# A two-layer decoder on one core: start-up loads reordered, first-batch rotary sums on VectorE, one projection step moved, and a new merge of the lanes

## Chip, cores and metric

One core of one Trainium2 chip. The metric is device time in microseconds (us) of one launch; the runs before are given as the median of 3. The engines are named as in the profile: PE is TensorE's matrix multiplication, PEld its weight load, DVE is VectorE, ACT is ScalarE, POOL is GpSimd, SP is SyncE; SPq and ACTq are the DMA issues of SP and ACT.

## What is computed

The input is 16 sequences (batches) of 256 tokens by 256 channels, float32, and a context of the same shape. Six residual blocks follow one another, each ended by a layer norm without weights:

```
x = LN(x + attention_16_heads_with_rotary(x))       # layer 0, attention 0
x = LN(x + mLSTM_like_mixer(q=x, k=ctx, v=ctx))     # gates, decay matrix, 8 heads
x = LN(x + bitlinear_ffn(x))                        # ternary weights, 8-bit activations
x = LN(x + attention_16_heads(x))                   # layer 1, attention 1
x = LN(x + cross_attention_16_heads(x, ctx, ctx))   # attention 2
x = LN(x + relu_ffn(x))
```

The rotary part turns each pair (x1, x2) of a head into (x1*cos - x2*sin, x1*sin + x2*cos). The ternary weights are made on the chip from float32 ones: each is divided by the mean of its absolute values, rounded, and clipped to -1, 0, 1.

## The kernel before

**Lanes.** The 16 sequences are spread over 4 lanes (L0 to L3), four batches to a lane, one after the other. Each lane has its own buffers; a fifth lane, SETUP, holds the start-up work that all share. One sequence is a fixed list of steps, written in `lane_steps()`: `ctx` and `xT` turn the context and the stream (PE transposes into PSUM, ACT copies out), `rope` projects queries and keys and multiplies them by cos and sin on DVE, `qk` splits them into two half-precision parts, `stack` reads them back stacked from DRAM, `max` makes the scores and DVE takes their row maxima (line 1170), `negmax` turns the maxima, `exp` makes the scores again and ACT exponentiates (line 999), `pv` multiplies by the values, `heads` turns the result, DVE normalizes it (lines 1181 and 1183), `oT` turns it back, `proj` projects it, and `norm` ends the block. A name is written here with its attention and its unit: `max 0.3 L2` is the fourth unit of attention 0 in lane 2.

**Order.** Every engine runs one list, a merge of the lanes' lists. The merges are written out by hand of a planner as strings of digits (`TURNS`, one digit a step, the lane that is next) and the PSUM bank of every PE result stands in `PLACES`. `engine_program()` reads them. Each engine waits on semaphores and takes its own steps strictly in order, so a step that isn't ready holds all that stand behind it, on SP too, which issues nearly all DMAs. `nth()` gives the count of a semaphore at which a step of a lane is done.

**Start.** SP issues the constants, then stream and context of the lanes by turns with the first weights between them, then waits for the context of lane 2 (`sp.wait_ge(c_loaded[2], 16)`), then issues the raw weights of the ternary layer (3 MB), the bias rows, and three weights of layer 1. ACT issues, before any of its steps, four DMAs that preset a slot of `heads_dram` (lines 940 to 942), and starts its steps only behind them. DVE sums the raw weights (`sums`, line 1123), makes the scales (`scales`, lines 1126 to 1131), the ternary values (`ternary`, lines 1137 to 1141) and the masks. SP's steps `weights 0` to `weights 4` load the other weights; each of 0 to 3 first waits for both stacks of the lane of its number, and they have 6, 8, 9 and 14 DMAs.

**First batch, order before.** Decoded from `TURNS`, with the steps of batch 0:

- SP behind the first loads: qk 0.0 L0, stack 0.0 L0, qk 0.1 L0, qk 0.0 L2, stack 0.1 L0, stack 0.0 L2, qk 0.0 L1, qk 0.1 L2, stack 0.0 L1, qk 0.1 L1, qk 0.0 L3, stack 0.1 L2, stack 0.1 L1, weights 0, weights 1, weights 2, stack 0.0 L3, qk 0.1 L3, negmax L0, stack 0.1 L3, negmax L2, negmax L1, weights 3, negmax L3, weights 4.
- PE: ctx L0, xT L0, v L0, ctx L3, xT L3, ctx L1, xT L1, rope 0 L0, rope 1 L0, ctx L2, xT L2, ... rope 0 L3, sums, rope 1 L3 ...
- DVE: rope 0 L0, rope 1 L0, sums, rope 0 L2, rope 0 L1, rope 1 L2, qk 0 L0, qk 1 L0, rope 1 L1, rope 0 L3, rope 1 L3, scales, qk 0 L2, ternary 2, qk 0 L1, qk 1 L1, qk 1 L2, max 0 L0 ... max 7 L3 (with the two qk of L3 between), ternary 0, ternary 1, masks, heads L0.

**Rotary sums.** DVE writes the products (line 1145, 128x512 each, two for each unit of 128 tokens). POOL adds them crosswise, in two instructions of 128x256 a unit (line 1340), into `R`, a view of the key buffer; 8 units in the first batch of the four lanes, 32 in all. POOL also adds a bias row to the stream once a block (`xb`, line 1345).

**Second attention of layer 1.** `v 2` (the values of the cross attention, from the context) stands behind `proj 1`; on DVE it waits for the last `pv` of attention 1, whose values lie in the same buffer.

Of the kernel before, what the change touches and what calls it, by code (L numbers as in the profile page):

```python
# [12 lines left out]
ALU = mybir.AluOpType  # L13
# [44 lines left out]
def lane_steps():  # L58
# [6 lines left out]
    def attention(a):  # L65
# [17 lines left out]
        if a == 1:  # L83
            add("qk", 2, 1)
            add("stack", 2, 1)
        add("oT", a)
# [3 lines left out]
        if a == 1:  # L90
            add("v", 2)
# [51 lines left out]
def lane_program(lane):  # L143
# [7 lines left out]
    for at in range(-1, batches):  # L151
        for name, occ, unit, ahead in lane_steps():
            it = at + ahead
            if 0 <= it < batches and (at >= 0 or ahead):
                out.append((it, name, lane, occ, unit))
# [6 lines left out]
        "0003311002231122200134322110000300302201120222211112121331323033033000103020222002022032022033023303"  # L162
        "3320123033211301011320110313102123013203012223100323123121233302231302302330211313111200000110100311"
        "3330213223123020232233302301001001120010102313310020031130132100330220002302120302303323003231310333"
        "0213233221213022132312202100232021023100112011120113013213233101030131030132021003222121322032303332"
        "0201203231130101101103100023220010003112130222320121312313300323311301310003002323202332000122100100"
        "2002222030133302033120133011321012022122312103011023330213330130330023030031100113211011022122322322"
        "3111211023311021132112311021002301303230332212321322130120301011222111111032232333300300230103013031"
        "3212022022003033200002010330131103211223103012333100332112332132023330213223321303123212212122311322"
        "0120200202302102110131231121031132312330100310110010010201223212230303203203213331231011100210130200"  # L170
        "2130320030110212113022021312333123002110323002103100303320320023123222100100022000322201330102233033"
        "1113113022122021213320101302332013303133300030230011132010113110021222322232132321321112011120331103"
        "1233121203231010023203132131022031201211220111321210003102333132013130100330332022202210030233120030"
        "1210001123013021002130321302123132023330233133232312131310323221230230220200232001232012212200210103"
# [1223 lines left out]
```

## Time and profile before

| what | value |
|---|---|
| median of 3 runs | 1826.56 us (1825.21 to 1827.41) |
| the profiled execution's own time | 1808.41 us |
| its span | 1806.7 us |
| PE busy | 1552.5 us, 86% of the span |
| DVE busy | 1180.4 us, 65% |
| ACT busy | 967.1 us, 54% |
| POOL busy | 227.1 us, 13% |
| mean granted TensorE clock | 0.962 of full speed |

All durations below are those of the profiled execution, counted from the start of its span. An "[idle before <-releaser]" names how long an engine had nothing to run before the row and what ended that wait. The share of PE is high in the mean, but the first 110 us are unlike the rest.

### The profile page before, as it was taken

What the parts mean: (1) busy time and instruction counts of PE and PEld (TensorE: products, weight loads), DVE (VectorE), ACT (ScalarE), POOL (GpSimd) and SP (SyncE); (2) the same over time, 40 slices, a digit from 0 to 9 for tenths busy, and PEclk for the clock granted to TensorE, in tenths of its full rate; (3) what the DMA queues carried; (4) which work ended last, traced back from release to release, by engine and by line L of the source; (5) the groups of instructions that cost most, each with busy time, mean ns of one, the idle gap of its engine ahead of it and who ended that gap; (6) DMA issues with size and microseconds to landing.
All of it is one profiled execution on the core that took longest, in us unless ns stands there. A gap on an engine that the chain in (4) does not pass through costs nothing. (4 is left out here: it accounts for less than half of the span.)

```text
span 1806.7 us, 31811 instructions
## 1 busy us (share of the span) xinstructions
PE 1552.5 (86%) x12524; PEld 998.1 (55%) x12546; DVE 1180.4 (65%) x2087; ACT 967.1 (54%) x1717; POOL 227.1 (13%) x233
## 2 busy tenths in 40 slices
PE   6389788879998887889999897888999989698898
PEld 4146455546664554545676465545566546464467
DVE  4856897664465678676447678876355668886732
ACT  2077554655435755456534664645544566555562
POOL 5200110002111011000122011000012111100000
PEclk9579899999999989999999999999999999999999
DMA  6610023221221011422122001232123101123200
GB/s 216 185 60 1 1 88 97 83 68 42 67 75 48 1 42 42 123 63 74 59 65 74 28 7 46 80 95 83 33 71 96 58 2 42 41 82 104 63 1 24
DMA packets 115748, 114.36 MB, mean 63 GB/s; under 512 B 10515, under 2 KB 101395, under 8 KB 115603
## 3 DMA queue, kind: packets, MB, share of 16 engines
q1 hardware_dynamic: 115282, 111.28, 20.1%
q8 instruction: 103, 1.69, 0.4%
q10 hardware_dynamic: 320, 1.05, 0.3%
q14 instruction: 43, 0.34, 0.1%
HBM read 68.91 MB, written 42.99 MB: 62 GB/s over the span
## 5 line engine op out<-in xcount | busy, mean ns | idle before, releaser
L1170 DVE TENSOR_REDUCE nm<-psum 128x4 f16<-128x1024 f32 x384 | 458.3, 1224 | 125.0 <-PE psum L760 123.0
L999 ACT ACTIVATE PB<-psum 128x1024 f32<-128x1024 f32 x384 | 383.9, 1023 | 229.5 <-PE psum L797 120.3
L1345 POOL TENSOR_TENSOR XO<-XO,row_b 128x512 f32<-128x512 f32 x80 | 101.5, 1276 | 1176.9 <-ACT XT L970 1155.6
L797 PE MATMUL psum<-PB,V 128*32 128x256 f32 x3072 | 211.5, 395 | 10.4 <-ACT PB L999 7.3
L760 PE MATMUL psum<-QK 48*128 48x256 f16 x1536 | 148.6, 288 | 77.2 <-DMA QK<-heads_dram 23.6
L779 PE MATMUL psum<-QK 49*128 49x256 f16 x1536 | 147.0, 280 | 42.5 <-ACT PB L999 20.4
L760 PEld LDWEIGHTS psum<-QK 48*128 48x128 f16 x1536 | 55.2, 97 | 166.5 <-issue 70.7
L797 PEld LDWEIGHTS psum<-PB,V 128*32 128x32 f32 x3072 | 84.5, 111 | 87.7 <-issue 36.8
L779 PEld LDWEIGHTS psum<-QK 49*128 49x128 f16 x1536 | 52.6, 95 | 137.8 <-issue 53.3
L924 PE MATMUL psum<-XT,W 128*128 128x256 f32 x512 | 120.1, 384 | 0.0
L932 PE MATMUL psum<-W,PB 128*128 128x256 f32 x512 | 116.7, 383 | 0.0
L1003 ACT ACTIVATE U<-psum 128x512 f32<-128x512 f32 x128 | 76.0, 596 | 55.4 <-PE psum L797 35.4
L924 PEld LDWEIGHTS psum<-XT,W 128*128 128x128 f32 x512 | 94.6, 190 | 18.7 <-issue 6.3
L932 PEld LDWEIGHTS psum<-W,PB 128*128 128x128 f32 x512 | 95.6, 190 | 16.5 <-issue 4.2
L1111 DVE TENSOR_SCALAR XO<-Y,mv,rstd 128x256 f32<-128x256 f32 x192 | 73.4, 426 | 43.2 <-ACT rstd L954 43.2
L687 PE MATMUL psum<-W_o,XT 128*128 128x256 f32 x384 | 96.3, 394 | 3.1 <-ACT XT L1006 1.8
L1340 POOL TENSOR_TENSOR QK<-PB 128x256 f32<-128x256 f32 x64 | 74.9, 1198 | 150.1 <-DVE PB L1145 150.0
L1083 ACT ACTIVATE PB<-psum,col_b 128x256 f32<-128x256 f32 x128 | 53.5, 471 | 73.0 <-PE psum L924 72.7
L674 PE MATMUL psum<-cst,XO 128*128 128x128 f32 x512 | 82.7, 286 | 10.6 <-DVE XO L1111 5.5
L1229 DVE SCALAR_TENSOR_TENSOR PB<-psum,PB 128x768 f32<-128x768 f32 x64 | 60.7, 953 | 42.2 <-PE psum L864 41.7
L687 PEld LDWEIGHTS psum<-W_o,XT 128*128 128x128 f32 x384 | 70.2, 192 | 20.7 <-issue 7.4
L1189 DVE TENSOR_TENSOR Y<-psum,XO 128x512 f32<-128x512 f32 x48 | 33.1, 689 | 71.5 <-PE psum L687 44.2
(158 smaller groups left out, 2582.6 us busy)
## 6 DMA issues: line engine op xcount, KB each, us to landing
QK<-heads_dram SPq DMA_DIRECT2D x96, 512.0 KB, 3.6
heads_dram<-U SPq DMA_DIRECT2D x288, 128.0 KB, 2.0
XO<-in_x SPq DMA_DIRECT2D x16, 256.0 KB, 3.3
Y<-in_ctx SPq DMA_DIRECT2D x16, 256.0 KB, 3.4
out<-XO SPq DMA_DIRECT2D x16, 256.0 KB, 3.4
W<-in_w SPq DMA_DIRECT2D x2, 1024.0 KB, 7.6
QK<-GN SPq DMA_DIRECT2D x96, 4.0 KB
heads_dram<-QK ACTq DMA_DIRECT2D x4, 256.0 KB, 9.1
```

Of the source, the lines that this page charges most:

```text
L674: ins = pe.transpose(bank[:, k * TOK + t * P:k * TOK + t * P + P], src[:, t, k * P:(k + 1) * P], ident)
L687: ins = pe.matmul(bank[:, t * DIM:(t + 1) * DIM], xt(k)[:, t * P:(t + 1) * P], w[:, k], start=(k == 0), stop=(k == n - 1))
L760: ins = pe.matmul(b[:, e * 512 + t * TOK:e * 512 + (t + 1) * TOK], QS[L][r, unit, t * P:(t + 1) * P], KS[L][r, unit, :], start=True, stop= ...
L779: ins = pe.matmul(b[:, e * 512 + t * TOK:e * 512 + (t + 1) * TOK], KS[L][r, unit, t * P:(t + 1) * P], QS[L][r, unit, :], start=True, stop= ...
L797: ins = pe.matmul(b[SLOT * j:SLOT * j + SLOT, at:at + TOK], value(L, t, PAIRS * e + u, HEADS, HD, SLOT), src, start=(t == 0), stop=(t == T ...
L924: ins = pe.matmul(b[:, m * TOK:(m + 1) * TOK], W_1[:, k, c:c + P], XT_[L][:, k, :], start=(k == 0), stop=(k == KT - 1))
L932: ins = pe.matmul(b[:, 0:DIM], hid1(L, k)[:, unit * P:(unit + 1) * P], W_2[:, k], start=(k == 0), stop=(k == IT - 1))
L999: act.activation(PB[L][:, unit % PBUF, :], b[:, 0:1024], ACT.Exp, scale=HD ** -0.5)\
L1003: act.activation(flat2(U[L][:, unit - 1:unit + 1, :]), b[:, 0:512], ACT.Copy).then_inc(u_ready[L], 1)
L1170: dve.tensor_reduce(nm[L][:, :, :, unit].rearrange("p t e -> p e t"), b[:, 0:1024].rearrange("p (e t k) -> p e t k", e=2, t=TT), AX.X, ALU ...
L1340: pool.tensor_tensor(both[:, two], plain[:, two], crossed[:, 1 - two], ALU.add).then_inc(rot[L], 1)
L1345: pool.tensor_tensor(stream(L, it), stream(L, it), row_b[:, occ:occ + 1, :].to_broadcast([P, TT, DIM]), ALU.add).then_inc(xb_ready[L], 1)
```

## The change

It has these parts:

- `first()` loads all four streams ahead of all four contexts, waits for the stream of lane 3 in place of the context of lane 2, and waits for two memsets of POOL (`set_pool` at 2).
- The four presets of `heads_dram` are issued by SP there, ahead of the raw weights, and no longer by ACT.
- In what runs ahead of batch 0, the `ctx` steps stand at the end, behind the stacks; `nth()` counts accordingly.
- For batch 0, DVE makes the rotary sums itself, right behind the products of the unit, and POOL skips them. Later batches are as before.
- `v 2` stands ahead of `oT 1` and `proj 1`, behind `stack 2.1`.
- `TURNS` and `PLACES` are replaced by a new merge with as many steps on each engine (PE 1905, ACT 1377, DVE 1014, SP 294, POOL 192).

```diff
         if a == 1:
             add("qk", 2, 1)
             add("stack", 2, 1)
+            add("v", 2)
         add("oT", a)
         if a == 2:
             add("loadx", 0, 0, 1)
         add("proj", a)
-        if a == 1:
-            add("v", 2)
...
-        for name, occ, unit, ahead in lane_steps():
+        steps = lane_steps()
+        if at < 0:
+
+            steps.sort(key=lambda step: step[0] == "ctx")
+        for name, occ, unit, ahead in steps:
...
+    if it == 0 and what in ("ctx", "xT0"):
+        return 1 + (what == "ctx")
     return it * len(signals) + signals.index(what) + 1
...
+        def turned_sums(engine, L, unit):
+            half = slice(512 * unit, 512 * unit + 512)
+            plain, crossed = (rot_t(L, n)[:, half].rearrange("p (c u two r) -> p two c r u", two=2, r=HD // 2, u=PAIRS)
+                              for n in range(2))
+            both = R[L][:, half].rearrange("p (c two r u) -> p two c r u", two=2, r=HD // 2, u=PAIRS)
+            for two in range(2):
+                engine.tensor_tensor(both[:, two], plain[:, two], crossed[:, 1 - two], ALU.add).then_inc(rot[L], 1)
...
                 load_x(0, 0)
-                load_c(0, 0)
                 load(qkv_loaded, (W_qkv[0][:, :, :], kt_major(w_qkv0)))
                 for L in range(1, LANES):
                     load_x(L, 0)
+                for L in range(LANES):
                     load_c(L, 0)
 
-                sp.wait_ge(c_loaded[2], 16)
+                sp.wait_ge(x_loaded[LANES - 1], 16)
+                sp.wait_ge(set_pool, 2)
+                load(slots_set, *[(heads_dram[L][:, :, 3].rearrange("j e r u t -> r (j e) (u t)"), last_rows) for L in range(LANES)])
                 load(raw_loaded, (raw[2].rearrange("p (k n) -> p k n", k=IT), kt_major(w_down)),
...
-            act.wait_ge(set_pool, 2)
-            load(slots_set, *[(heads_dram[L][:, :, 3].rearrange("j e r u t -> r (j e) (u t)"), last_rows) for L in range(LANES)])
             act.wait_ge(set_pool, 4 + 2 * LANES)
...
+                    if it == 0:
+                        dve.wait_ge(rot_parts[L], 2 * unit + 2)
+                        turned_sums(dve, L, unit)
...
                 if name == "rope":
-                    pool.wait_ge(rot_parts[L], it * 4 + 2 * unit + 2)
...
+
+                    if it:
+                        pool.wait_ge(rot_parts[L], it * 4 + 2 * unit + 2)
+                        turned_sums(pool, L, unit)
```

**First batch, order after**, decoded from the new `TURNS`:

- SP behind the first loads: qk 0.0 L0, stack 0.0 L0, qk 0.1 L0, qk 0.0 L2, stack 0.1 L0, qk 0.0 L1, stack 0.0 L2, weights 0, qk 0.1 L2, stack 0.0 L1, stack 0.1 L2, qk 0.0 L3, qk 0.1 L1, stack 0.1 L1, stack 0.0 L3, qk 0.1 L3, weights 1, weights 2, stack 0.1 L3, negmax L2, negmax L0, weights 3, negmax L1, negmax L3, weights 4.
- PE: xT L0, v L0, rope 0 L0, xT L1, rope 1 L0, v L1, rope 0 L1, xT L3, xT L2, v L2, v L3, rope 0 L3, rope 0 L2, qk 0 L0, sums, qk 1 L0, rope 1 L2, ctx L0, rope 1 L1 ...
- DVE: rope 0 L0, rope 1 L0, rope 0 L1, sums, rope 0 L2, qk 0 L0, rope 1 L2, qk 1 L0, rope 1 L1, qk 0 L2, scales, rope 0 L3, qk 0 L1, qk 1 L2, rope 1 L3, max 0 L0, max 1 L0, ternary 2, qk 1 L1, max 2 L0 ... max 7 L3, ternary 0, ternary 1, masks, heads L0.

On PE, 403 of the 1905 steps keep their exact position, half move by no more than one, and 101 by more than five. Counted in steps of PE, and averaged over the 16 sequences, `proj 1` stands 9.4 steps behind `heads 1` before and 11.5 after, and the first `max` of attention 2 stands 40.4 and 40.8 steps behind `heads 1`.

## Rows read from the trace of the kernel before

**Rows 1.** Windows view, busy us (x instructions) of each engine, PEclk, DMA share, GB/s.

```profile
0.00:110.00 110.00, 65.45 (x370) 35.17 (x374) 77.04 (x79) 28.15 (x41) 34.21 (x45) 0.74 0.57 172
110.00:500.00 390.00, 339.34 (x2852) 217.92 (x2849) 248.55 (x462) 227.64 (x402) 42.45 (x42) 0.98 0.19 59
500.00:900.00 400.00, 347.28 (x2914) 222.86 (x2918) 272.95 (x486) 223.10 (x397) 46.71 (x46) 0.98 0.19 57
900.00:1300.00 400.00, 350.87 (x2828) 222.12 (x2834) 272.19 (x486) 218.02 (x394) 46.94 (x46) 0.96 0.19 58
1300.00:1700.00 400.00, 353.88 (x2877) 229.11 (x2882) 271.79 (x494) 222.12 (x398) 50.53 (x49) 0.98 0.20 61
...
sum 1807.00, PE 1552.49 PEld 998.13 DVE 1180.42 ACT 967.13 POOL 227.07; mean PE 221.78 PEld 142.59 DVE 168.63 ACT 138.16 POOL 32.44
```

**Rows 2.** Windows view of one late 10 us of the start.

```profile
100.00:110.00 10.00, 8.80 (x78) 3.14 (x78) 8.45 (x12) 7.69 (x10) 0.00 (x0) 0.52 0.28 57
```

**Rows 3.** Timeline of DVE from 20 to 110 us: start, us, group, [idle before].

```profile
25.49 1.29 DVE L1145 TENSOR_TENSOR PB<-psum,cst 128x512 f32<-128x512 f32 x2 [19.86 <-PE psum L720]
...
28.41 4.47 DVE L1123 TENSOR_REDUCE w_scale<-W 128x1 f32<-128x2048 f32 x2
...
37.47 3.68 DVE L1145 TENSOR_TENSOR PB<-psum,cst 128x512 f32<-128x512 f32 x6 [2.39 <-PE psum L720]
...
46.92 1.01 DVE L1129 TENSOR_TENSOR w_k<-w_scale 128x1 f32<-128x1 f32 x1
47.96 1.19 DVE L1131 TENSOR_TENSOR w_k<-w_k,w_scale 128x1 f32<-128x1 f32 x1
...
49.67 1.69 DVE L1137 TENSOR_SCALAR W_gu<-W_gu,w_scale 128x2048 f32<-128x2048 f32 x1
...
55.44 1.87 DVE L1153 TENSOR_TENSOR U<-psum,U 128x512 f16<-128x512 f32 x3
...
68.05 1.23 DVE L1170 TENSOR_REDUCE nm<-psum 128x4 f16<-128x1024 f32 x1 [1.62 <-PE psum L760]
...
90.89 9.25 DVE L1170 TENSOR_REDUCE nm<-psum 128x4 f16<-128x1024 f32 x8 [3.05 <-PE psum L760]
100.05 1.27 DVE L1137 TENSOR_SCALAR W<-W,w_scale 128x2048 f32<-128x2048 f32 x1
...
103.77 1.28 DVE L1137 TENSOR_SCALAR W<-W,w_scale 128x2048 f32<-128x2048 f32 x1
...
108.44 0.14 DVE L1119 TENSOR_SCALAR nb_g<-b_g 40x1 f32<-40x1 f32 x1
```

**Rows 4.** Timeline of PE: the first exp step, and heads 0 of lane 0.

```profile
93.31 0.61 PE L779 MATMUL psum<-QK 49*128 49x256 f16 x4 [1.18 <-DVE nm L1170]
...
115.39 1.09 PE L808 MATMUL psum<-cst,U 128*128 128x128 f32 x8
```

**Rows 5.** Timeline of all engines, 0 to 20 us.

```profile
4.41 6.02 ACTq L942 DMA_DIRECT2D heads_dram<-QK  x4
...
17.30 0.37 SPq L576 DMA_DIRECT2D W_gu<-in_w_down  x1
...
19.43 1.11 PE L674 MATMUL psum<-cst,Y 128*128 128x128 f32 x4 [3.98 <-DMA Y<-in_ctx]
```

**Rows 6.** Tile view of XO, ns min/median/max: a DVE sum of 128x256.

```profile
L1197 DVE TENSOR_TENSOR Y<-psum,XO x32: 414/424/426, 428.5 to 1801.2; 128x256 f32<-128x256 f32 x32
```

**Rows 7.** The page's costliest groups: POOL's rotary sums.

```profile
L1340 POOL TENSOR_TENSOR QK<-PB 128x256 f32<-128x256 f32 x64 | 74.9, 1198 | 150.1 <-DVE PB L1145 150.0
```

**Rows 8.** Timeline of SP's queue: the issues of weights 1 and 2.

```profile
68.79 10.55 SPq L576 DMA_DIRECT2D W_o<-in_w_proj  x16
```

**Rows 9.** Groups of PE instructions from 110 to 1800 us.

```profile
L760 PE MATMUL psum<-QK 48*128 48x256 f16 x1408 | 131.4, 277 | 53.0 <-ACT PB L999 16.8 <-DMA QK<-heads_dram 12.0 <-DVE nm L1170 8.4
...
L687 PE MATMUL psum<-W_o,XT 128*128 128x256 f32 x384 | 96.3, 394 | 3.1 <-ACT XT L1006 1.8 <-ACT PB L999 0.8 <-DVE U L1153 0.2
L674 PE MATMUL psum<-cst,XO 128*128 128x128 f32 x496 | 78.9, 283 | 10.6 <-DVE XO L1111 5.5 <-DVE XO L1183 2.2 <-DVE Y L1254 1.3
```

More of the change, by code:

```diff
@@ L167 @@
[L167 to L171, printed above, removed]
@@ new lines @@
+        "1212032021210102112111110032010332020333211301031333022203022000200320230013013012121321230010331030"
+        "2211133202333220323312331311231133012323113220122203020022231201211021212110213131331032130213110031"
+        "0230020223002120102323330233113122111101333013223021011220201231211232112110123121310131323120121223"
+        "32211"),
+    "act": (
+        "0132031200402221113330201200001030202220002202303222330302333021330311132001131002113122301330212220"
+        "0331331122312233300021311120331023011120003302130202133021233012323311121012001120001100010003000330"
+        "3330233303330322332223222222312322131201110111021121120011013000310011333023033203222033000100302022"
+        "1300211132220023101311233311333233212013232302022122001000021000022101011011030113103033300133312333"
+        "0230003020122323022231312202111323101121110213320130223013322122011320303102101122311311323323221333"
+        "2031213002200010200000211021211230012331033330133110333033323223222322321222212212011111120211120100"
+        "0111300010001031303333323033020020103003122100110232220132201311233323112333323201102302213222002200"
+        "1002000102211010110130110330103323001333133032030032022320130222322201312331110211102332111312333012"
+        "0222201103102011331002113221111323333223113120332120032120002100021000212021120003111013303330333333"
+        "2333223222222322322032212001001211121112111111130010033133310020303333022022000130000230011222311222"
+        "0123130023113111233332133321033220022200022100020000122010110113101103300133003213331333030002320022"
+        "2302322132221301323111210110331112323120213322220031101020313011222113101113323332123311230232002000"
+        "1202003001021212201001201310133103330333133323332322223122322221213111222111021111020211100030100300"
+        "10103333233322033313022012012202011122321121311112003131121332331222111022321"),
@@ L1333, in _ @@
                 if name == "rope":
-                    pool.wait_ge(rot_parts[L], it * 4 + 2 * unit + 2)
-                    half = slice(512 * unit, 512 * unit + 512)
-                    plain, crossed = (rot_t(L, n)[:, half].rearrange("p (c u two r) -> p two c r u", two=2, r=HD // 2, u=PAIRS)
-                                      for n in range(2))
-                    both = R[L][:, half].rearrange("p (c two r u) -> p two c r u", two=2, r=HD // 2, u=PAIRS)
-                    for two in range(2):
-                        pool.tensor_tensor(both[:, two], plain[:, two], crossed[:, 1 - two], ALU.add).then_inc(rot[L], 1)
+                    if it:
+                        pool.wait_ge(rot_parts[L], it * 4 + 2 * unit + 2)
+                        turned_sums(pool, L, unit)
                 elif name == "xb":
```

116 lines of the change are left out of this document (50 added, 66 removed).

## Prediction

> **What bounds the kernel now.** I read the windows first, to see which engine sets the pace of each stretch. Over the whole span PE is busy 1552.5 of 1807 us, but not evenly [rows 1]. From 110 to 1700 us it is busy 339.3 of 390, 347.3, 350.9 and 353.9 of 400 us: four stretches, each about one batch of all lanes, in which PE lacks 50.7, 52.7, 49.1 and 46.1 us. There PE is the bound, and what is lost is many small waits, no single one. In the first 110 us it is busy only 65.5 us, at a mean granted clock of 0.74; DVE has 77.0 us there. Late in that stretch the granted clock is 0.52, the lower of the two levels (1.2 GHz) [rows 2].
>
> The timeline of DVE says why [rows 3]. DVE's first rotary product starts at 25.5 us, behind 19.9 us of idling. From 28.4 us, when the raw weights are there to be summed, to 108.6 us, the end of the masks, DVE has 80.2 us, and its large waits in them are only 2.4, 1.6 and 3.1 us. PE's first exp step is at 93.3 us and the heads of lane 0 are turned at 115.4 us [rows 4], just behind DVE's last start-up work. So the start is DVE's: whatever shortens the stretch from 28.4 to 108.6 us should move the rest of the program forward, since the order behind it is fixed and PE sets its pace.
>
> **The change, part by part.**
>
> *Loads and presets.* Before, ACT issues four presets from 4.4 to 10.4 us and can't copy a transpose until then; SP holds the raw weights back until 17.3 us, when lane 2's context is in; and PE, whose order puts the context of lane 3 second, stands until 19.4 us [rows 5]. After, ACT is free at once, lane 0 needs only its stream and the first weights, and contexts come later. Some 1.9 MB (constants, weights, four streams) are ahead of SP's wait in place of some 3.7 MB (those, three contexts and the presets). By bytes, my estimate is that the wait ends at 17.3 x 1.9 / 3.7, about 9 us, and 10 with some latency. The presets then cost SP at least 4 issues of 0.4 us and at most the 6.0 us they took on ACT [rows 5], so the raw weights are issued between 12 and 16 us. The same bytes still have to move ahead of them or beside them, so their landing gains less than their issue: between 0 and 3 us, and I take 1. Behind these waits on SP stand the raw weights, bias rows, three weights of layer 1 and all head traffic, none of which is wanted before the raw weights are in. The memset wait costs nothing, since ACT's issues, behind the same wait, began at 4.4 us.
>
> *What lies ahead of the stretch.* With the streams in early, both units of lane 0 and the first of lane 1 can be multiplied and summed before the raw weights land, where 19.9 us were idle. Lane 1's unit leaves the bound stretch: -1.3 us of products.
>
> *The sums on DVE.* 16 instructions move, 6 of them ahead of the stretch, 10 into it. The trace has no DVE sum of this access pattern from buffer to buffer. The nearest row is DVE's 128x256 float32 sum at 0.42 us [rows 6]; the far end is POOL's own 1.20 us for these very sums [rows 7]. I take 0.42, the same engine and size: +4.2 us; the far end is +12. POOL's other start-up work, four stream additions, goes earlier and costs nothing.
>
> *What POOL leaves free.* While POOL sums, DVE is slow: three passes over 128x2048 take 5.8 us (49.67 to 55.44) and the same three take 3.7 us without POOL (100.05 to 103.77), and two sums of one column take 1.0 and 1.2 us [rows 3]. With POOL gone, -2.1 us, and about -1.9 us for the two small ones (to some 0.15 us each): -3.9 us with rounding, and between 0 and that. Together with the +4.2 and -1.3, DVE's work in the stretch changes by -1.0 us.
>
> A rule of the Trainium skill speaks against counting all of it ("SBUF — State Buffer", the section on the two separate sides): DVE operations with two SBUF inputs and GpSimd operations that read SBUF take one port pair for a whole instruction each, and the other waits. The slow small sums agree with it. It is a rival below.
>
> *Waits in the stretch.* The 3.1 us before lane 3's maxima are those in which SP was issuing 10.6 us of weights 1 and 2 ahead of lane 3's first stack [rows 3, 8]. In the new order they stand behind it, and only its second stack waits for them, while DVE has lanes 1 and 2 to reduce: gone. The 2.4 us before the third rotary unit came from the late streams: gone too. Late next is SP's weights 0, which now waits for lane 0's two stacks with lane 2's second half behind it, and weights 3 ahead of lane 1's negmax. I give 2.5 of the 5.5 us back to them: -3.0 us, with bounds 0 and -7.
>
> *Contexts last.* Four transposes of PE and four copies of ACT move into the stretch, where PE is busy under two thirds of the time: 0, and if that cover fails some 4.4 us (four times the 1.1 us of the row at 19.43) [rows 5].
>
> *v 2 ahead of proj 1.* PE does the same work. The waits it could fill are small: between 110 and 1800 us PE stood 2.2 us for the heads that oT needs and 1.8 us for the turned heads that proj needs [rows 9]. In the new merge proj 1 stands two steps later but the next attention's first max no later (40.8 steps against 40.4). I take 0; bounds are -4 and the slower rival below.
>
> *The new merge.* As many steps on each engine, half of PE's moved by at most one place. I take 0. As bounds I use what four differently merged batches cost now: PE lacks 46.1 to 52.7 us in 400 [rows 1]. Were all four like the best, -14 (four times 46.1 against 198.6); like the worst, +12.
>
> **Sum.** -1.0 (weights in) -1.0 (work) -3.0 (waits) = -5.0 us. The profiled execution took 1808.4 us by itself, so 1803.4 us for one like it. That execution is 18.2 us below the median of the runs; I carry the difference over unchanged: 1826.6 - 5.0 = 1821.5 us. About 0.2% (3.7 us) is what a measurement of this kernel can tell from no change.
>
> **Rivals.**
>
> *A. The start's gain is given back (1826.5 us).* SP stops at weights 0 until lane 0's second stack has landed, then issues six DMAs, with lane 2's second half and both stacks behind; DVE runs dry before lane 2's maxima. Or the sums cost 1.2 us and the work grows by 8. Either takes the 5 us. For it: SP's order is strict and the stalls now seen are of this kind. Against it: DVE has six maxima and ternary 2 to do meanwhile.
>
> *B. The port (1826.5 us).* Four stream additions of POOL meet the moved sums and hold each other for up to a full instruction each, some 1.3 us: +5. Here the rule named above would leave the start where it was. Against it: POOL is idle most of the time, and the meetings must fall on the same moments.
>
> *C. A longer chain (slower, about 1837 us).* v 2 is 8 matmuls, 2.0 us by the projections' rate (96.3 us for 384) [rows 9], and it now stands between a lane's heads and its proj 1, norm, xT 3, qk, stack and max. PE already waits 12.0 us for stacks read from DRAM and 53.0 us in all before its max steps [rows 9]. If half of the 16 sequences pass it on, that is +16, and with the -5 it makes +11. It decides from five of them on: 5 x 2.0 = 10 us eats the 5 us and the bound of 3.7. For it: two more steps between heads and proj. Against it: the total distance to max is unchanged.
>
> *D. A better merge (about 1810 us).* The batches all come out near the best of those now, -10 on top of the start.
>
> That the change doesn't do what it says is small: the only parts that could be void are the SP waits.
>
> **From cases to numbers.** Forecast 0.45, with a range of its own from 1816 to 1822.5; A 0.18; B 0.07; C 0.20; D 0.10. Faster is the forecast and D: 0.55; same is A and B: 0.25; slower is C: 0.20. The range from 1811 to 1832 holds the forecast, A, B, half of D and a third of C. Each of the start's terms at its own end, the others as taken, lies in it too: the sums at 1.2 us make +2.8 in all, no POOL gain -1.1, all waits gone -9.
>
> **What would show it.** In the changed kernel's profile: DVE's first rotary product well before 19 us, not at 25.5; the first summing of raw weights near 27 us; DVE's sums at 0.42 us each under a new line; three passes over 128x2048 at 3.7 us both times; no wait of 3 us before lane 3's maxima; DVE's masks ending near 104 us, not 108.6, and lane 0's heads near 110 us. From there PE should lack about 199 us to 1700 us, as now. The forecast is wrong if the masks end where they did, if heads follow later than the masks by more than now, or if PE's lack in the four stretches moves by more than 5 us either way.

## Result and the profile after

In the same series of runs, the kernel before took 1821.49 us (median of 20 runs, 1813.29 to 1832.87) and the changed kernel 1828.42 us (20 runs, 1817.02 to 1835.40). The ratio is 1.0035 with a 95% interval of [1.0018, 1.0051]: 0.35% slower, where 1821.5 against 1826.56 had been forecast, 0.28% faster. It lies inside the range of 1811 to 1832, but on the other side of before than the forecast. Here and below, a few executions in a second, slower state are left out of the ratios and intervals; the one profiled of the new start with the old order behind it (1912.8 us) was among them, so no line of that profile is read.

The profiled execution took 1825.37 us (span 1823.6 us, mean granted clock 0.945); the one of before took 1808.41 us at 0.962. The windows of the changed kernel, in the columns of [rows 1]:

```profile
0.00:110.00 110.00, 64.02 (x358) 34.14 (x358) 81.20 (x94) 27.21 (x39) 13.42 (x29) 0.71 0.61 170
110.00:500.00 390.00, 342.75 (x2842) 219.54 (x2839) 250.95 (x464) 224.32 (x400) 42.93 (x42) 0.96 0.19 59
500.00:900.00 400.00, 346.23 (x2794) 216.20 (x2802) 265.59 (x477) 215.51 (x382) 44.30 (x44) 0.93 0.17 52
900.00:1300.00 400.00, 348.33 (x2868) 223.27 (x2870) 272.67 (x488) 221.97 (x398) 47.15 (x46) 0.97 0.21 63
1300.00:1700.00 400.00, 357.96 (x2858) 234.03 (x2855) 266.53 (x485) 220.37 (x400) 52.87 (x51) 0.97 0.19 57
```

PE's clock and busy time differ. From 500 to 900 us PE is as busy as before (346.2 against 347.3 us), but gets through 2794 matmuls instead of 2914, at a granted clock of 0.93 instead of 0.98 [rows 1]. And PE's lack over the four stretches is 47.3 + 53.8 + 51.7 + 42.0 = 194.7 us, less than the 198.6 of before. The whole span says it again: PE is busy 1570.4 us where it was 1552.5 [rows 1], +17.9 us, and idle 253.2 us where it was 254.2 (span less busy time). So in this pair of profiles the loss is not PE waiting longer, but the same work taking longer at a lower clock. The pair overstates it, though: the two executions are 17 us apart where the medians are 6.9, because the profiled execution of before is the fastest of that kernel on record.

DVE's timeline in the start, beside [rows 3]:

```profile
13.42 1.29 DVE L1154 TENSOR_TENSOR PB<-psum,cst 128x512 f32<-128x512 f32 x2 [7.79 <-PE psum L735]
14.74 1.09 DVE L465 TENSOR_TENSOR QK<-PB 128x256 f32<-128x256 f32 x2
...
31.98 4.48 DVE L1132 TENSOR_REDUCE w_scale<-W 128x1 f32<-128x2048 f32 x2 [10.54 <-DMA W<-in_w_up]
...
43.76 1.29 DVE L1154 TENSOR_TENSOR PB<-psum,cst 128x512 f32<-128x512 f32 x2 [2.19 <-PE psum L735]
...
49.95 0.13 DVE L1138 TENSOR_TENSOR w_k<-w_scale 128x1 f32<-128x1 f32 x1
50.11 0.16 DVE L1140 TENSOR_TENSOR w_k<-w_k,w_scale 128x1 f32<-128x1 f32 x1
...
58.28 1.27 DVE L1146 TENSOR_SCALAR W_gu<-W_gu,w_scale 128x2048 f32<-128x2048 f32 x1
...
60.85 1.23 DVE L1150 TENSOR_SCALAR W_dn<-W_gu 128x2048 bf16<-128x2048 f32 x1
...
90.32 11.52 DVE L1182 TENSOR_REDUCE nm<-psum 128x4 f16<-128x1024 f32 x10 [3.70 <-PE psum L775]
...
110.14 0.14 DVE L1128 TENSOR_SCALAR nb_g<-b_g 40x1 f32<-40x1 f32 x1
117.33 0.36 DVE L1193 RECIPROCAL rs<-psum 128x32 f32<-128x32 f32 x1 [7.05 <-PE psum L823]
```

The first product comes at 13.4 us instead of 25.5, the two small sums take 0.13 and 0.16 us instead of 1.0 and 1.2, and the three passes end 3.8 us after they begin. But DVE then stands 10.5 us for the raw weights, which it sums from 31.98 us and not from 28.41; a wait of 3.7 us is left before the last maxima; and the masks end at 110.3 us, not at 108.6.

These last two ends can't be told apart by one profile each. Eight profiles were taken of kernels with the old order up to PE step 630 at least, before itself twice among them: their last mask instruction begins between 108.4 and 113.0 us, and the heads of lane 0 are normalized between 115.7 and 121.5 us. Three of the start as changed (two come from the experiments on `v 2` below) have 110.1 to 110.9 and 117.3 to 120.3 us. The late weights are clear of that spread: the sum of the raw weights starts at 28.2 to 29.2 us in the eight and at 32.0 to 32.2 in the three. The issues of SP say why the weights are late:

```profile
10.46 5.24 SPq L589 DMA_DIRECT2D heads_dram<-QK  x4
15.73 2.58 SPq L589 DMA_DIRECT2D W_gu<-in_w_down  x1
18.36 2.77 SPq L589 DMA_DIRECT2D W<-in_w_gate  x1
21.18 0.49 SPq L589 DMA_DIRECT2D W<-in_w_up  x1
...
72.99 11.00 SPq L589 DMA_DIRECT2D W_o<-in_w_proj  x16
...
84.57 0.39 SPq L659 DMA_DIRECT2D QK<-heads_dram  x1
```

The presets hold SP for 5.2 us, and the first two issues behind them take 2.6 and 2.8 us each, where one took 0.37 [rows 5]. The last raw weights are issued at 21.2 us. The DMA engines aren't idle meanwhile, but they move little. The windows view of the changed kernel, its last two columns being the DMA share and GB/s:

```profile
14.00:18.00 4.00, 4.00 (x15) 2.51 (x14) 3.93 (x8) 0.45 (x1) 0.00 (x0) 1.00 0.95 100
22.00:26.00 4.00, 4.00 (x16) 2.78 (x15) 0.00 (x0) 1.57 (x3) 0.00 (x0) 1.00 1.01 294
```

While the presets are under way (7.5 us from issue to landing in the median), the engines are 95% busy at 100 GB/s; behind them the raw weights move at 294. PE pays for the late weights too, because its own step `sums` stands in order and has to wait for DVE's:

```profile
PE psum L714 <- DVE w_scale L1132: 10.6, 1, 10.6
```

(In the list of waits the columns are total, number and longest, in us.) The wait of 3.7 us before the last maxima is PE's wait for lane 3's second stack, which SP issues at 84.57 us, behind the 11 us of `weights 1` and `weights 2`:

```profile
89.67 1.04 PE L775 MATMUL psum<-QK 48*128 48x256 f16 x8 [4.65 <-DMA QK<-heads_dram]
```

### The profile page after: what moved, and what is told of

Read it like the earlier page. It is cut to its first block, busy times and chain, and to the rows that moved or that the text cites. A ratio compares the mean times of both kernels' runs of the same rounds, so it can differ in the third digit from the quotient of the medians.

```text
span 1823.6 us, 31784 instructions
## 1 busy us (share of the span) xinstructions
PE 1570.4 (86%) x12525; PEld 1006.6 (55%) x12546; DVE 1186.3 (65%) x2103; ACT 967.3 (53%) x1717; POOL 207.0 (11%) x217
## 4 chain that ended last, share of the span: by engine, by line
PE 52%; DVE 12%; ACT 8%; DMA 4%; issue 3%; SPq 1%; POOL 0%; DVEq 0%; ACTq 0%
PE psum L702 8%; PE psum L812 7%; PE psum L947 6%; PE psum L939 6%; PE psum L695 4%; DVE nm L1182 4%; ACT PB L1008 4%; PE psum L794 3%; PE psum L775 3%; DMA heads_dram<-U 3%; PE psum L689 2%; PE psum L735 2%; PE psum L823 2%; DMA QK<-heads_dram 2%; PE psum L879 1%
## 5 line engine op out<-in xcount | busy, mean ns | idle before, releaser
L794 PEld LDWEIGHTS psum<-QK 49*128 49x128 f16 x1536 | 51.7, 95 | 131.6 <-issue 52.8
L1120 DVE TENSOR_SCALAR XO<-Y,mv,rstd 128x256 f32<-128x256 f32 x192 | 79.7, 460 | 32.1 <-ACT rstd L963 31.8
L689 PEld LDWEIGHTS psum<-cst,XO 128*128 128x128 f32 x512 | 58.9, 145 | 48.9 <-issue 28.6
L702 PEld LDWEIGHTS psum<-W_o,XT 128*128 128x128 f32 x384 | 71.6, 196 | 20.3 <-issue 6.8
```

The lines of the kernel that those rows point to most:

```text
L689: ins = pe.transpose(bank[:, k * TOK + t * P:k * TOK + t * P + P], src[:, t, k * P:(k + 1) * P], ident)
L702: ins = pe.matmul(bank[:, t * DIM:(t + 1) * DIM], xt(k)[:, t * P:(t + 1) * P], w[:, k], start=(k == 0), stop=(k == n - 1))
L794: ins = pe.matmul(b[:, e * 512 + t * TOK:e * 512 + (t + 1) * TOK], KS[L][r, unit, t * P:(t + 1) * P], QS[L][r, unit, :], start=True, stop= ...
L1120: dve.tensor_scalar(stream(L, it)[:, t], Y[L][:, t], mv[L][:, t, 0:1], rstd[L][:, t:t + 1], ALU.subtract, ALU.mult).then_inc(x_ready[L], 1)
```

## Experiments

All ratios are to the kernel before, from the same series of runs, with 95% intervals. "Old" and "new" are the orders (`TURNS`, `PLACES`, place of `v 2`) of before and after. A kernel that joins the two gives each engine the steps of the first piece in the order of one, then the rest in the order of the other; the pieces are cut at a step of PE, and each lane's steps are divided at the same point on all engines. Everything is computed in all of them.

### Start and rest apart

In the code of these kernels "A" is the new order and "B" the old one. The first has the new start up to PE step 84 and the old rest; the second has the two letters exchanged.

```diff
+START, REST, CUT, SETUP_ALL = "A", "B", 84, True
...
+def engine_program(engine):
+    ...
+    return ([s for s in order_of(START, engine) if s in FIRST] + [s for s in order_of(REST, engine) if s not in FIRST])
```

> The new start (loads, presets, sums on DVE, contexts last, new order up to the first 84 steps of PE), and behind it the order and PSUM places of before, with v 2 behind proj 1. Theory 1 (the time went in the rest: the new merge has more short waits of PE, each followed by some microseconds at the lower clock): about as before or 1 us above it, ratio 0.999 to 1.001, granted clock as before's own. Rival (the time went in the start, which ended 0.8 us later and at a lower clock): all of the loss is here, ratio about 1.0035.

> The start of before, and behind it the new merge with v 2 ahead of proj 1. Theory 1 (loss in the rest): ratio about 1.003, granted clock lower than before's. Rival (loss in the start): ratio about 1.000. If both hybrids lose, the loss is spread, or comes from chance in where the clock falls.

The new start with the old rest gave 1.0008 [0.9981, 1.0034], 1825.79 us; the old start with the new rest 1.0043 [1.0021, 1.0065], 1830.95 us. The start is worth nothing either way, within 0.3%; the loss is in the rest.

### The presets back on ACT

```diff
                 sp.wait_ge(x_loaded[LANES - 1], 16)
-                sp.wait_ge(set_pool, 2)
-                load(slots_set, *[(heads_dram[L][:, :, 3].rearrange("j e r u t -> r (j e) (u t)"), last_rows) for L in range(LANES)])
...
+            act.wait_ge(set_pool, 2)
+            load(slots_set, *[(heads_dram[L][:, :, 3].rearrange("j e r u t -> r (j e) (u t)"), last_rows) for L in range(LANES)])
             act.wait_ge(set_pool, 4 + 2 * LANES)
```

> The changed kernel with the four presets issued by ACT again. Theory S (SP's 5.2 us of preset issues and the slow issues behind them made the raw weights land at 32.0 us, not 28.4): raw weights are summed from about 28 us, DVE's masks end about 3.5 us earlier than 110.3 us, lane 0's heads likewise, and the time falls by about 3 us, ratio 0.998 to the changed kernel. Rival (the weights are late because the DMA engines are full with the contexts, whoever issues the presets): landing stays near 32 us.

> The new start with the presets issued by ACT again, and the order of before behind it. If the two findings add (the rest of before costs nothing more than before, and presets on ACT gave 0.3% against the changed kernel): ratio to before 0.997 to 0.999, weights summed from 28.4 us, masks ended near 107 us. If DVE's masks are not what sets the pace up to the first heads: no gain, 1.000 to 1.001.

The changed kernel with this edit gave 1.0007 [0.9983, 1.0030], 1824.25 us; the new start with the old rest and this edit 0.9971 [0.9940, 1.0002], 1817.48 us. Timelines of SP and DVE in the first:

```profile
14.25 0.37 SPq L589 DMA_DIRECT2D W_gu<-in_w_down  x1
14.66 1.70 SPq L589 DMA_DIRECT2D W<-in_w_gate  x1
16.40 1.06 SPq L589 DMA_DIRECT2D W<-in_w_up  x1
```

```profile
28.38 4.48 DVE L1136 TENSOR_REDUCE w_scale<-W 128x1 f32<-128x2048 f32 x2 [6.64 <-DMA W<-in_w_up]
...
107.12 0.14 DVE L1132 TENSOR_SCALAR nb_g<-b_g 40x1 f32<-40x1 f32 x1
115.97 0.36 DVE L1197 RECIPROCAL rs<-psum 128x32 f32<-128x32 f32 x1 [8.70 <-PE psum L821]
```

The raw weights are in 3.6 us sooner (28.38 for 31.98), the masks end 3.0 us sooner and the heads come 1.4 us sooner. All three profiles with the new start and the presets on ACT (this one, the one with the old order behind it, and the last kernel below) have the sum at 27.6 to 28.4 us and the last mask instruction at 103.8 to 107.1, ahead of every profile of the old start (108.4 at the earliest). So the presets, where the change put them, cost the start 3 us at the masks in the pair that differs in nothing else. The edit moves two things at once, the queue of the presets and their time (ACT issues them from 4.4 us, SP did from 10.5), and these aren't told apart. In both pairs the edit took about 0.3% off (1.0035 to 1.0007, 1.0008 to 0.9971), but each pair is across two series of runs and the intervals overlap in both, so the 0.3% is not shown by them.

### Scores three times

```diff
-                    for t in range(TT):
+                    for t in (list(range(TT)) * (3 if (it, occ) == (0, 0) else 1)):
```

> The changed kernel with the score matmuls of max in the first batch's attention 0 made three times into the same PSUM place (32 steps, 256 more matmuls, same result). Theory 2 (PE's clock falls in the start because PE has little to do, and what follows pays for it): the granted clock from 60 to 110 us rises to near 1, exp and pv of the first batch run at the higher level, lane 0's heads come 4 to 8 us earlier. Rival (PE's clock in the start costs nothing, DVE sets the pace up to 110 us): heads within 1 us of 117.3, or up to 20 us later if PE stays at the lower level and three times 0.6 us exceeds DVE's 1.15 us a step.

It gave 1.0068 [1.0042, 1.0094], 1837.63 us; by the two ratios that is 0.33%, some 6 us, above the changed kernel. Windows view, then DVE's timeline:

```profile
0.00:110.00 110.00, 74.61 (x580) 48.78 (x581) 76.97 (x86) 23.29 (x34) 13.43 (x29) 0.78 0.60 170
```

```profile
115.91 0.14 DVE L1128 TENSOR_SCALAR nb_g<-b_g 40x1 f32<-40x1 f32 x1
122.55 0.36 DVE L1193 RECIPROCAL rs<-psum 128x32 f32<-128x32 f32 x1 [6.51 <-PE psum L823]
```

The granted clock of the start went up from 0.71 to 0.78 with the additional matmuls, but PE was busy 10.6 us longer, the masks ended 5.8 us later and the heads 5.2 us later. More than half of the additional PE time reached the end of the start. So PE's idle time there is only partly room for more work, and a higher clock bought with additional matmuls doesn't pay for them here. From 60 to 110 us, which the expectation was about, the clock rose from 0.53 to 0.63 only and not to near 1, so what a full clock in that stretch would be worth wasn't tried.

### The place of v 2 alone

```diff
+            v = (it, "v", L, 2, 0)
+                out.remove(v)
...
+                out.insert(at, v)
```

In the old merge it goes ahead of `oT 1` (early), in the new one behind `proj 1` (late); everything else stays. In the first two, ACT's order moves with it; in the second two only PE's and DVE's, with DVE's turn three PE steps behind PE's.

> The kernel before, with its own merge and start, and only v 2 taken ahead of oT 1 and proj 1 (16 steps moved on PE and DVE, each in a free PSUM bank). Theory V (the values ahead of the second projection lengthen every lane's chain, my rival C): ratio to before about 1.004, as much as the whole change. Theory M (it is the merge, the order of all the other steps, and not this step): within 0.2% of before.

> The changed kernel with its new merge and start, and only v 2 put back behind proj 1. Theory V: the loss goes, ratio to before about 1.000. Theory M: it stays, 1.003 to 1.006.

> The kernel before with v 2 taken ahead of oT 1, two steps of PE ahead of it, and on DVE behind the steps whose PE part is up to three behind, as the new merge has it. In the first try DVE's place for it was nearer to PE's, and cost 2%. Theory V (the step's place makes the change slower): 1.003 to 1.005. Theory M (the order of the rest does): 0.999 to 1.001. A planless move that disturbs its neighbours: above 1.01, and then nothing can be told of the step itself.

> The changed kernel with v 2 put back four steps of PE behind proj 1, and on DVE with the same lag of three. Theory V: 1.000 to 1.001 against before. Theory M: 1.003 to 1.006. Disturbed neighbours: above 1.01.

Measured: early in the old merge 1.0198 [1.0156, 1.0240] and 1.0266 [1.0228, 1.0304]; late in the new merge 1.0205 [1.0164, 1.0245] and 1.0250 [1.0221, 1.0279]. Moving the step by hand costs 2% and more in both directions. Both directions can't be slower because of the place alone, since one undoes the other. That it is the price of a step and a PSUM bank put into a merge that wasn't made for them is my reading, which no run tests. These four say nothing about which place is better; one step can't be judged alone here.

### Where in the merge

Each pair is an order and the PE step up to which it holds (`None` is the end); one line is one kernel. The first two are written in the form of the experiment on start and rest. The last expectation is that of the kernel before, profiled once more without an edit.

```diff
+START, REST, CUT, SETUP_ALL = "B", "A", 770, True
+START, REST, CUT, SETUP_ALL = "B", "A", 1010, True
+PIECES = [('B', 630), ('A', None)]
+PIECES = [('B', 84), ('A', 770), ('B', None)]
+PIECES = [('B', 630), ('A', 770), ('B', None)]
```

> The kernel before up to its first 770 steps of PE (about 740 us), the new merge with v 2 ahead of proj 1 behind them. Theory W (the loss of the new merge sits in one stretch, from about 740 to 1000 us, where the changed kernel falls 20 us behind the profile of before, and everywhere else it is even): ratio about 1.003 to 1.005, granted clock near 0.942. Rival (the loss is spread over the whole rest): half of it or less, ratio about 1.002.

> The kernel before up to its first 1010 steps of PE (about 960 us), the new merge behind them. Theory W: within 0.1% of before, or a little faster, granted clock near 0.950. Rival (spread): ratio about 1.002, clock about 0.947.

> The kernel before up to its first 630 steps of PE (about 615 us), the new merge behind them. Theory R (the loss sits in the new order of steps 630 to 770, about 615 to 760 us, behind which the changed kernel's dips lie; behind step 770 the new merge gains): ratio 1.001 to 1.004, granted clock near 0.943, and 10 us or more behind before at 790 us. Rival E (the loss sits earlier, in steps 84 to 630): 0.996 to 0.998, as with the cut at 770.

> The kernel before with the new merge only from step 84 to step 770 of PE. If parts add: the whole rest new is 1.0043, from 770 on it is 0.9968, so this one should be 1.0043 + 0.0032 = 1.0075, and the slowest of the pieces. If they don't add (what follows a loss absorbs it), about 1.004.

> The kernel before with the new merge only from step 630 to 770 of PE. Theory R: 1.003 to 1.007. Rival E: 1.000.

> The kernel before, unchanged, for a second profile. Theory K (the clock dips are partly chance: the same program shows more or fewer of them from run to run, and its time moves along by about 1 us for each 0.001 of mean granted clock): a time and clock on the same line as the runs of the changed kernel, for instance 1823 us at 0.947. Rival (the dips are fixed by the program): clock again 0.962 and time again near 1808 us.

| order | ratio | 95% interval | median, us |
|---|---|---|---|
| new behind step 1010 | 0.9953 | [0.9931, 0.9975] | 1813.66 |
| new behind step 770 | 0.9968 | [0.9944, 0.9991] | 1818.38 |
| new behind step 630 | 1.0033 | [1.0006, 1.0061] | 1826.27 |
| new from 630 to 770 only | 1.0064 | [1.0035, 1.0093] | 1832.87 |
| new from 84 to 770 only | 1.0097 | [1.0060, 1.0133] | 1838.08 |

The new merge is better behind step 770 and worse before it. The 140 steps from 630 to 770, some 615 to 760 us of the span, cost 0.64% by themselves. A second profile of the kernel before (own time 1812.56 us, span 1811.0, clock 0.959) shows where, beside that of the kernel with the new order in these steps only (span 1829.6). DVE's timeline, the heads of attention 1, lane 0, and the next heads; before again:

```profile
735.94 0.34 DVE L1181 RECIPROCAL rs<-psum 128x32 f32<-128x32 f32 x1
768.11 0.35 DVE L1181 RECIPROCAL rs<-psum 128x32 f32<-128x32 f32 x1
```

and new from 630 to 770:

```profile
736.08 0.35 DVE L1308 RECIPROCAL rs<-psum 128x32 f32<-128x32 f32 x1
...
781.65 0.36 DVE L1308 RECIPROCAL rs<-psum 128x32 f32<-128x32 f32 x1 [0.32 <-PE psum L935]
```

At the same time at 736 us and 13.5 us late at the next, and 15 to 20 us late from there to the end. In the changed kernel the same delay stands: against the first profiled execution of before its heads are 3.3 us late at this point, 11.0 at the next, 15.5 at the one after.

The heads at 736 us mislead, because the two orders have done unlike amounts of work by then: since the heads ahead of these (616.7 and 617.4 us) PE has made 774 matmuls in the old order and 734 in the new. From those heads to the ones at 768 and 782 us the work is the same again. Windows over just that stretch, of before again, of new from 630 to 770, and of the two kernels of the next section (630 to 730, 730 to 770):

```profile
616.70:768.11 151.41, 124.30 (x1008) 82.29 (x1011) 118.64 (x236) 84.82 (x159) 16.84 (x19) 0.98 0.20 58
617.39:781.65 164.26, 132.54 (x1009) 85.43 (x1008) 119.82 (x236) 84.95 (x159) 16.89 (x19) 0.91 0.19 57
618.53:779.59 161.06, 131.46 (x1008) 85.02 (x1011) 118.90 (x236) 85.06 (x159) 16.83 (x19) 0.92 0.18 56
618.62:778.70 160.08, 131.07 (x1005) 85.13 (x1008) 119.62 (x236) 84.57 (x159) 16.87 (x19) 0.92 0.20 58
```

The same 1008 matmuls take 12.9 us longer in the new order: PE is busy 8.2 us longer, at 0.91 for 0.98, and idle 4.6 us longer. The first profile of before has 154.2 us here, busy 128.1 at 0.94, so 3 us of such a difference can be chance. Windows of 20 us, before again:

```profile
680.00:700.00 20.00, 15.01 (x103) 10.68 (x103) 16.42 (x42) 6.96 (x16) 3.86 (x4) 0.98 0.17 44
...
760.00:780.00 20.00, 16.92 (x150) 10.14 (x150) 15.03 (x21) 8.53 (x15) 1.27 (x1) 1.00 0.46 146
```

new from 630 to 770:

```profile
680.00:700.00 20.00, 14.08 (x79) 9.29 (x80) 15.41 (x35) 4.76 (x12) 3.88 (x4) 0.66 0.00 1
...
760.00:780.00 20.00, 15.11 (x110) 8.64 (x110) 10.80 (x13) 7.81 (x14) 1.27 (x1) 0.85 0.55 165
```

and the changed kernel:

```profile
680.00:700.00 20.00, 15.12 (x81) 10.24 (x81) 14.27 (x31) 5.15 (x13) 3.89 (x4) 0.74 0.07 21
```

From 680 to 700 us PE is busy about as long, but makes 79 or 81 matmuls in place of 103, at a clock of 0.66 or 0.74 in place of 0.98. This dip isn't the whole loss, nor sure to belong to the new order: over 660 to 700 us the clock is 0.91 in before again, but 0.83 in the first profile of before, as in these two kernels, and the costliest kernel of the table (84 to 770) has 0.91. PE's timeline there, before again:

```profile
680.92 1.91 PE L687 MATMUL psum<-W_dn,U 128*128 128x256 bf16 x16
...
692.24 1.99 PE L680 MATMUL psum<-XT,W_qkv 128*128 128x256 f32 x8
```

and new from 630 to 770:

```profile
685.51 3.45 PE L814 MATMUL psum<-W_dn,U 128*128 128x256 bf16 x16
...
693.66 1.08 PE L801 MATMUL psum<-cst,XO 128*128 128x128 f32 x4 [3.36 <-DVE XO L1238]
695.53 3.64 PE L807 MATMUL psum<-XT,W_qkv 128*128 128x256 f32 x8 [0.78 <-ACT XT L1097]
```

The sixteen matmuls of the down projection take 3.45 us instead of 1.91, and the eight of a projection 3.64 instead of 1.99, which is the lower of the two clock levels. Between them PE waits 3.4 us for the layer norm of the lane whose stream it has to turn, where it waits 1.3 us in the old order.

### The stretch split once more

```diff
-PIECES = [('B', 630), ('A', 770), ('B', None)]
+PIECES = [('B', 630), ('A', 730), ('B', None)]
...
+PIECES = [('B', 730), ('A', 770), ('B', None)]
```

> The order of before throughout, but PE steps 630 to 729 (and the steps of the other engines that belong to them) in the new merge; the two kernels of this call split the stretch that cost 1.0064 by itself. Theory (it is the reordering between heads 1 of lane 0 and the exps of lane 3, where the delay showed between the heads at 731 and at 764 us): 0.999 to 1.002 here, and no delay of over 2 us at heads number 17. Rival (it begins with the converted projections at the halved clock near 685 to 700 us): 1.005 to 1.008 here, with a granted clock of 0.66 or so from 680 to 700 us.

> The order of before throughout, but PE steps 730 to 769 in the new merge. There the new merge puts down 0 of lane 1, qk 2.1, v 1 of lane 2 and v 2 of lane 0 between the scores and the first exp of lane 3. Theory: 1.005 to 1.008, and 8 to 14 us late at heads number 17 (764 us), on time at number 16. Rival: 0.999 to 1.002. If both kernels come out between 1.002 and 1.005, the loss is of the stretch as a whole and of no place in it.

Measured 1.0040 [1.0001, 1.0080], 1826.78 us, and 1.0056 [1.0031, 1.0081], 1831.78 us. Both halves cost something, so no single place does it. The first is 10.6 us late already at the heads at 736 us, with the 774 matmuls of the old order behind it; from 680 to 700 us it has a clock of 0.66 as well. The second is on time there, but with 730 matmuls done, and 10.6 us late at the next heads. Over the same 1008 matmuls as above they take 9.7 and 8.7 us longer than before again, and the joint kernel 12.9. PE's timeline of the second, just ahead of them:

```profile
769.54 0.39 PE L887 MATMUL psum<-QK 48*128 48x256 f16 x4 [1.58 <-DVE U L1283]
772.96 0.61 PE L887 MATMUL psum<-QK 48*128 48x256 f16 x4 [3.03 <-DMA QK<-heads_dram]
773.50 1.93 PE L924 MATMUL psum<-PB,V 128*32 128x256 f32 x16
```

PE waits twice, 1.6 us for DVE's `U` and 3.0 us for a stack from DRAM, and then come matmuls at the lower level (sixteen of this form take 1.07 us elsewhere in this trace, 1.93 here). Of the steps that the expectation lists ahead of lane 3's first `exp`, only `v 2` of lane 0 is new there; the others stood ahead of it in the old order too, and `oT 1` of lane 0 went behind it. The theory held for this kernel in size and in where the delay shows. For its partner it didn't: 1.004 and a delay of 10.6 us were measured where it said up to 1.002 and none.

### A version that beats both

New start, old order from PE step 84 to 1010, new order behind it, and the presets on ACT as above:

```diff
+PIECES = [('A', 84), ('B', 1010), ('A', None)]
```

> The parts that gained, together: the new start with the presets on ACT, the order of before up to step 1010, the new merge with v 2 ahead of proj 1 behind it. If they add: 0.9971 and 0.9953 make 0.992 to 0.994, about 1809 to 1812 us. If each gain is the same slack: about 0.995.

It gave 0.9907 [0.9877, 0.9937], 1805.34 us (6 runs): 0.93% below the kernel before, where 0.992 to 0.994 was expected if the gains add. DVE's timeline in its start:

```profile
27.56 4.48 DVE L1260 TENSOR_REDUCE w_scale<-W 128x1 f32<-128x2048 f32 x2 [1.31 <-DMA W<-in_w_up]
...
103.77 0.14 DVE L1256 TENSOR_SCALAR nb_g<-b_g 40x1 f32<-40x1 f32 x1
112.09 0.36 DVE L1321 RECIPROCAL rs<-psum 128x32 f32<-128x32 f32 x1 [8.19 <-PE psum L945]
```

Weights from 27.6 us, masks to 103.9 us. The heads are 6.4 us earlier than in the second profile of before in the first batch, still 5 to 6 us earlier from 736 to 950 us, and the last ones 13.2 us earlier. PE is busy 1563.8 us and idle 239.1, where it was 1552.9 and 258.1: 19 us less waiting, of which 11 come back as busy time in this pair. That execution of before was again a fast one (1812.56 us, clock 0.959). Over the runs the mean clock is 0.955 with the joined order and 0.953 before, so this kernel wins by waiting less and not by its clock.

## Why the prediction was wrong

**The step that failed: "The new merge ... I take 0".** It had the widest bounds of all terms, and I had priced it by counts and by mean places. Its cost from step 84 to 770 is +0.97%, some 17 us, its worth behind step 770 -0.32%, some 6 us; together +12, and the new rest as a whole +8 (1.0043), near the +12 that stood in the prediction as the far bound. The bound was argued from PE's lack, though, and the lack went down by 3.9 us. What rose was PE's busy time, with the granted clock at 0.943 on average over 20 runs where it had been 0.952. That the merge lowers the clock by where it puts short waits is argued from a few places and not shown. Nor is all of the merge's cost clock: with the new order from 630 to 770 only, the clock is lower by 0.0046 and the time longer by 12.9 us (means over 12 and 23 runs), and at 1.1 us for each 0.001, as the 23 runs of before in that series have it, 5 us of them go with the clock. The other 8 us don't; that profile has PE idle 4.6 us longer in the stretch. My test ("if PE's lack in the four stretches moves by more than 5 us either way") couldn't have seen it.

**The start, forecast -5.0 us, gave nothing: 1.0008 [0.9981, 1.0034].** The forecast of 0.28% faster rested on it alone, and the signs named for it (masks near 104 us, heads near 110) didn't come. With the presets on ACT the masks come at 103.9 to 107.3 us and the heads at 112.1 to 116.0. So it failed in the part on loads and presets and in the waits, as follows. That the measured time still fell into the range is due to the range's width.

**Raw weights in: forecast -1.0, measured +3.6 us.** The forecast said that the issues begin between 12 and 16 us; SP began them at 15.7, and issued the last at 21.2. The presets took 5.2 us, inside my bounds of 1.6 and 6.0, but the issues behind them took 2.6 and 2.8 us each, for which the sum had nothing. With the presets on ACT the sum starts at 28.38 us, which is what it was before: of the gain I gave to "fewer bytes ahead" nothing shows in that kernel, and 0.9 us in the best one (27.56).

**The sums: forecast 0.42 us each, measured 0.54.** Two of them take 1.09 us (0.58 each by itself, slightly overlapped). Ten in the stretch make +1.2 us more than forecast; the near row was the right one to lean to, the far one (1.20 us) was not.

**What POOL leaves free: forecast -3.9, held.** Three passes in 3.8 us instead of 5.8, and two small sums in 0.3 us instead of 2.2: -3.9. The rule of the Trainium skill that two-input DVE operations and GpSimd's SBUF reads exclude each other ("SBUF — State Buffer", the section on the two separate sides) agrees with this: with POOL's rotary sums gone, a two-input operation of one column costs 0.13 us and not 1.0. The three passes have one tensor input each, so this part of the rule doesn't speak of them; the trace shows only that they are fast without POOL beside them. Rival B, which expected the rule to cost 5 us at the four stream additions, wasn't put to the test: POOL made all four from 34.3 to 39.2 us, and none of DVE's sums fell there (the nearest are at 20.3 and 39.9 us).

**Waits in the stretch: forecast -3.0, measured -1.9.** From the raw weights' sum to the end of the masks it was 80.2 us and is 78.3. DVE is busy 71.9 and 72.0 us of it, so the work changed by nothing where -1.0 was forecast (the sums took the 1.2 us more), and all of the -1.9 is idle time, 8.3 us before and 6.4 after. But it isn't the waits I had named that went: the 2.4 us became 2.2 and the 3.1 us became 3.7, while the 1.6 us before a single maximum and a few short ones went. The step "only its second stack waits for them, while DVE has lanes 1 and 2 to reduce: gone" was wrong. `weights 1` and `weights 2` stand behind lane 3's first stack now (SP issues them from 73 us), its second stack is issued behind them at 84.6, PE stands 4.65 us for it, and DVE has run out of maxima by then. PE is a limit there too, as the run with the scores three times shows: 5.8 of 10.6 us that PE was given in addition arrived at the masks. So the cover that I named for the four context transposes was thinner than "busy under two thirds".

**v 2: open.** Rival C (a longer chain, slower by 11 us) had the sign of the result, but nothing shows its mechanism. The orders that put `v 2` early behind step 770 or 1010 are faster than before, so with them in the new merge the place doesn't cost 2 us a sequence there. From step 730 to 770 early values are part of what was moved, with other steps; they weren't separated from it.

**The base.** I made the sum against a profiled execution 18 us below the median, and carried the difference over as if it were noise around a fixed program. The clock goes with it: 0.962 in that execution, 0.952 on average over 32 runs of the same kernel. The profile of before had shown the kernel at its luckiest. For the sum this did no harm, since the 5 us were taken off the median; in the end the median over 20 runs, 1821.5 us, equalled the forecast of 1821.5 for the changed kernel, which is chance.

**What stays open.** Which of the reorderings within steps 630 to 729 and 730 to 769 does it, and why the two halves together (1.0064; 12.9 us in the profiled stretch) cost less than the sum of the two (1.0040 and 1.0056; 9.7 and 8.7 us), for which the intervals are too wide. Also how much of the 0.97% of steps 84 to 770 lies before 630: the difference of 0.33% is within the two intervals.

## What to carry to other kernels

Where PE is the bound, split its span into busy and idle and compare both: a new order can leave PE's idle time as it was and still lose, with the same matmuls at a lower granted clock. Compare milestones only where the same work lies ahead of them, and profile the same start more than once before a difference of 2 us in it is read: here it moved by over 4 us between profiles of the same order. Price a new merge by running its pieces in the old one, not by counts of steps; here one part of it was worth keeping and one was not, and the best kernel has both ends of the new order and the middle of the old. A DMA issue isn't a fixed price: behind the presets on SP's queue it took 2.6 us in place of 0.37.

## What was not expected of the hardware

- **Time follows the mean granted clock, run by run.** Over 32 runs of the kernel before in one series, the times fall by 0.97 us for each 0.001 of the mean granted clock (correlation -0.77; mean 1822.7 us at 0.9522). Over 20 runs of the changed kernel it is 1.15 us (correlation -0.92), from 1817.02 us at 0.952 to 1835.40 at 0.935. The difference of the two means, some 0.0094 in the clock, would make 9 to 11 us at that rate; 6.9 us between the medians were measured. From one kernel to another the rate doesn't carry: the changed kernel with the presets on ACT is 2.0 us above before in the mean at a clock lower by 0.0090, and new from 630 to 770 is 12.9 us above it at 0.0046.
- **A wait of a few us in a dense stretch goes with the lower clock level around it.** Behind the 3.4 us wait at 690 us eight matmuls took 3.64 us in place of 1.99; behind the 3.0 us wait at 773 us sixteen took 1.93 in place of 1.07. In these two places the wait and the slow matmuls behind it come together. That isn't a rule for each wait: the down projection ahead of the first was slow already.
- **SP's issues behind the presets.** 2.58 and 2.77 us each for one DMA of 1 MB, where the same two issues took 0.37 and 0.58 us before and 0.37 and 1.70 us with the presets on ACT's queue. The DMA engines were 95% busy at 100 GB/s while the presets moved, and moved 294 GB/s behind them.
